# A graph layer's per-step node row, loaded as one row and spread by TensorE

## The reference

```
rel_t_enc = cos((last_update[src] - t)[:, None] * time_w + time_b)
e = concatenate([rel_t_enc, msg]) @ We                   # per edge
q = (x @ Wq + bq)[dst];  k = (x @ Wk + bk)[src] + e
alpha = sum(q * k, per head) / sqrt(64)
a = softmax of alpha over the edges of one dst
out = segment_sum((v[src] + e) * a, dst) + x @ Wskip + bskip
x = layernorm(x + out)
```

## Time and profile before

| | us |
|---|---|
| median of 3 runs | 12,685.32 (12,684.47 to 12,685.91) |
| profiled execution, its own time | 12,758.32 |
| its span, first to last instruction | 12,756.5 |
| busy in the span: POOL / PE / DVE / ACT | 9104.8 / 8280.4 / 7035.3 / 4268.4 |

### The profile page before, as it was taken

The page is one execution under the profiler, slowest core; times in us unless marked ns, Lnnn a source line. Parts: engine busy times, 40 slices in busy tenths (PEclk is TensorE's granted clock), DMA queues, the critical chain, the costliest instruction groups (busy, mean ns, idle before and its releaser), DMA issues.

```text
span 12756.5 us, 215589 instructions
## 1 busy us (share of the span) xinstructions
PE 8280.4 (65%) x44603; PEld 7400.1 (58%) x44604; DVE 7035.3 (55%) x23935; ACT 4268.4 (33%) x14084; POOL 9104.8 (71%) x7644
## 2 busy tenths in 40 slices
PE   5777777777777777777645555555555555555555
PEld 2666666666666666666635555555555555555555
DVE  4776776777777777767763333333333333333334
ACT  1444444444444444444422222222222222222221
POOL 2666666666666666666468888888888888888884
PEclk8777877787777777777766666666666666666667
DMA  6555555555555555555533333333333333333335
GB/s 184 150 149 146 148 149 149 148 152 148 150 148 148 150 152 150 148 149 149 135 37 35 35 35 35 35 35 35 35 35 35 35 35 35 35 35 35 35 35 120
DMA packets 1699357, 1205.64 MB, mean 95 GB/s; under 512 B 749995, under 2 KB 1471983, under 8 KB 1699023
## 3 DMA queue, kind: packets, MB, share of 16 engines
q0 software_dynamic: 634368, 675.42, 32.8%
q1 hardware_dynamic: 1013840, 503.68, 15.2%
q10 hardware_dynamic: 51072, 25.69, 0.7%
HBM read 924.83 MB, written 279.22 MB: 94 GB/s over the span
## 4 chain that ended last, share of the span: by engine, by line
DMA 22%; issue 20%; POOL 19%; DVE 13%; another core or an unknown queue 9%; PE 8%; DVEq 4%; SPq 3%; ACT 2%; POOLq 0%; ACTq 0%
DMA part_scratch<-kve,idx 21%; POOL part_scratch L609 19%; DVE y_all L1142 3%; PE bank L703 2%; DVE acc L1275 2%; PE bank L694 1%; DVEq L375 1%; PE bank L684 1%; DVEq L273 1%; PE bank L676 1%; DVE ohT L1135 1%; ACT wv L859 1%; DVE oh L1188 1%; DVE oh L1181 1%
## 5 line engine op out<-in xcount | busy, mean ns | idle before, releaser
L609 POOL DMA_INDIRECT part_scratch<-kve,idx x3232 | 5134.7, 1589 | 1056.8 <-issue 884.2
L560 POOL DMA_INDIRECT kv<-kv_scratch,took x3520 | 3544.5, 1007 | 2303.4 <-issue 1366.8
L761 PE MATMUL bank<-ident,kv 128*128 128x128 f32 x3232 | 753.4, 377 | 2403.8 <-DVE ohT L1364 2314.6
L1390 DVE TENSOR_TENSOR idx<-kv,twins 128x4 int32<-128x4 f32 x808 | 131.4, 163 | 3627.2 <-DMA part_scratch<-kve,idx 3627.2
L761 PEld LDWEIGHTS bank<-ident,kv 128*128 128x128 f32 x3232 | 489.4, 188 | 2582.1 <-ACT kv L940 2217.7
L859 ACT ACTIVATE wv<-tables,weights 128x65 f32<-128x65 f32 x7040 | 1771.5, 337 | 3.5 <-PE bank L703 2.5
L771 PE MATMUL bank<-ohT,oh 128*128 128x128 f32 x6464 | 1644.2, 435 | 148.6 <-DVE oh L1356 138.8
L771 PEld LDWEIGHTS bank<-ohT,oh 128*128 128x128 f32 x6464 | 1408.1, 321 | 423.7 <-DVE oh L1356 357.0
L947 ACT ACTIVATE oh<-bank 128x512 f32<-128x512 f32 x808 | 482.4, 597 | 3258.4 <-PE bank L771 3258.3
L703 PE MATMUL bank<-wv,oh 128*128 128x130 f32 x7040 | 1302.3, 342 | 363.4 <-issue 239.3
L1123 DVE TENSOR_TENSOR tables<-kv,bank 128x512 f32<-128x512 f32 x880 | 599.7, 681 | 1682.1 <-remote 1610.8
(11 more groups left out here) (166 smaller groups left out, 9952.4 us busy)
## 6 DMA issues: line engine op xcount, KB each, us to landing
kve<-nodes_scratch SPq DMA_DIRECT2D x880, 256.0 KB
feat<-in_edge_attr_dram SPq DMA_DIRECT2D x880, 96.0 KB
kv<-kv_scratch,took POOLq DMA_INDIRECT x3520
qb<-q_scratch SPq DMA_DIRECT2D x880, 64.0 KB
part_scratch<-kve,idx POOLq DMA_INDIRECT x3232
part_scratch<-zrow SPq DMA_DIRECT2D x220, 128.0 KB
feat<-in_edge_attr_dram SPq DMA_DIRECT2D x880, 32.0 KB
kv<-part_scratch ACTq DMA_DIRECT2D x56, 448.0 KB, 6.0
```

The source lines that it names most:

```text
L560: pool.indirect_dma_start(kv[:, k, g, :], None, kv_d, bass.IndirectOffsetOnAxis(ap=took[:, j, g, 0:1].bitcast(I32), axis=0)).then_inc(s_ga ...
L609: pool.indirect_dma_start(part_d[g], bass.IndirectOffsetOnAxis(ap=idx[:, k, g:g + 1], axis=0), sum_ring[:, k, g, :], None, compute_op=ALU. ...
L761: op = pe.transpose(banks[0][:, g * P:(g + 1) * P], taken[:, st.k, 0, g:g + 1].to_broadcast([P, P]), ident[:, :])
```

## The change

SP loads the node row once, as 512 floats on one partition (`row_in`, two slots in `kve`). PE multiplies a row of ones with it (`row_stage`, one matmul of 512 columns, one ahead of what was the most advanced stage), so that all 128 partitions of a PSUM bank hold the row; ACT copies the bank to `node_row_of` (`rowc_stage`), which now has two slots; DVE's `onehotT_stage` waits for ACT's copy where it waited for the DMA. The PSUM bank comes from the node sums, which keep `banks[6]` alone. PE's sum for a step now waits for DVE's sum of the step just before. Two lists are reordered: PE's `sum_stage` comes after `q_stage`, and DVE's `sum_stage` comes right after `ke_stage`, not last.

```
-                wait(sp, s_oht, st.before(QS))
-                sp.dma_start(node_row_of[:, r, :], nodes_d[...].rearrange("(a n) -> a n", a=1).to_broadcast([P, G * P])).then_inc(s_bc[r], 16)
+                wait(sp, s_row, st.before(2))
+                sp.dma_start(row_in[:, st.k % 2, :], nodes_d[...].rearrange("(a n) -> a n", a=1)).then_inc(s_bc[st.k % 2], 16)
...
+            def row_stage(st):
+                pe.wait_ge(s_bc[st.k % 2], 16 * st.use(2))
+                wait(pe, s_rowc, st.s)
+                pe.matmul(row_ps[:, :], ones[0:1, :], row_in[:, st.k % 2, :], start=True, stop=True).then_inc(s_row, 1)
...
-                wait(pe, s_acc, st.before(2))
+                wait(pe, s_acc, st.s)
...
-                    at(i, k, (feat_stage, 15), (sum_stage, 1), (q_stage, 14), (e_stage, 15))
+                    at(i, k, (feat_stage, 15), (q_stage, 14), (sum_stage, 1), (e_stage, 15), (row_stage, 16))
...
+            def rowc_stage(st):
+                act.wait_ge(s_row, st.s + 1)
+                wait(act, s_oht, st.before(2))
+                act.activation(node_row_of[:, st.k % 2, :], row_ps[:, :], ACT.Copy).then_inc(s_rowc, 1)
...
-                    at(i, k, (featc_stage, 15), (weigh_stage, 2), *sines, *gaps, *exps, *smalls)
+                    at(i, k, (featc_stage, 15), (weigh_stage, 2), *sines, *gaps, *exps, *smalls, (rowc_stage, 16))
...
-                dve.wait_ge(s_bc[r], 16 * st.use(QS))
+                dve.wait_ge(s_rowc, st.s + 1)
...
-                    at(i, k, *turn[0], (ve_stage, 14), *turn[1], (ke_stage, 14), *turn[2], (block_stage, 0), *once(5, forward_stage),
+                    at(i, k, *turn[0], (ve_stage, 14), (block_stage, 0), *turn[1], (ke_stage, 14), *turn[2], (sum_stage, 0), *once(5, forward_stage),
```

More of the change, by code:

```diff
@@ L218, in build @@
         e_ps, q_ps = banks[2:4], banks[4:6]
-        agg_ps = [banks[6 + j][:, 0:HEADS * HB] for j in range(2)]
+        agg_ps, row_ps = banks[6][:, 0:HEADS * HB], banks[7]
         mT_ps, small_ps = banks[0][:, 0:G * ROWS], banks[0][:, 128:128 + 4 * ROWS]
```

17 lines of the change are left out of this document (9 added, 8 removed).

## The result

| | before | after |
|---|---|---|
| median | 12,685.61 us (12,684.47 to 12,686.27, 4 runs) | 12,904.44 us (12,900.53 to 12,911.75, 4 runs) |
| ratio | 1 | 1.0173, 95% interval 1.0156 to 1.0191 |
| profiled execution's span | 12,756.5 us | 12,909.9 us |

The change costs 219 us, or 0.25 us on each of the 880 steps. The direction was forecast; the size was not: the forecast of 13,300 us meant 615 us more than before, 2.8 times what was measured. The profiled execution of before lies 73 us above its median and that of after 7 us above, and the two spans are only 153 us apart; I take sizes from the medians and use the traces for the places.

What follows compares the result with a forecast made beforehand. It took the DVE-PE exchange between gather bursts as the bound. Terms 0.4 + 0.7 + 0.3 = 1.4 us per two steps, 616 us over 880 steps, gave 13,300 us; forecast range 12,900 to 13,650, 8-in-10 range 12,600 to 13,900.

Steps and rivals of the forecast that it cites:

- the feat term: On PE, feature transposes queued behind the row may miss the open part: 1.7 to 2.5 us if so, 0.7 taken.
- period of two steps: POOL gathers two steps in a burst, then the next burst starts: 13.94 us; the forecast added 1.4 us to it.
- The e term: On PE, e starts 1.4 to 2.3 us later, behind DVE's and PE's sums; 0.4 us per period taken.
- 0.74 us of room: Slack between ke's end with POOL's wake-up and POOL's fifth gather, said to absorb part of DVE's 0.6 to 1.5 us loss.
- the open part: Time between gather bursts when PE's results reach other engines promptly and SP's loads start 0.54 us apart.
- second reading: Check of the sum: 6.4 us of PE work and 1.2 to 1.3 us of remaining waits, 7.6 to 7.7 a step.
- The ACT term: On ACT, the row's copy queues ahead of the feature copy PE needs: 0 to 0.6 us per period, 0.3 taken.
- release: Moment a gather burst is through and DVE and ACT, held waiting for PE's results, start at once.
- The SP term: SP waits for PE's row matmul two steps back, with other loads queued behind; costed at 0.
- The closed parts: While gathered rows are in flight, PE's results reach others late and queues creep; SP's loads were 2.86 us apart.
- the door: Image for prompt delivery of PE's results: a gather burst closes it until about 2 us after its last gather's start.
- Rival (c): PE's 1.92 us of idle time takes the row in, so nothing changes: 12,685, at worst some 20 us more; chance 0.10.

Runs made afterwards that it cites:

- one_bank: Kernel before with one PSUM bank for the node sums and both changed orders (PE, DVE), row still broadcast: 12,839.66 us, 1.0043.
- order_only: Kernel before with both changed orders, PE's and DVE's, but two banks for the sums: 12,830.22 us, 1.0043.
- bank_matmul: one_bank plus one spare 512-column matmul a step on PE, waiting for nothing and read by nobody: 12,872.03 us, 1.0145 of the kernel before.
- bank_copy: bank_matmul plus ACT's copy of that bank and the two waits between PE and ACT: 12,886.81 us, 1.0155 of the kernel before.
- four_slots: Changed kernel with four places for the loaded row instead of two, so SP waits for the matmul four steps back: 12,860.85 us, 1.0139 of the kernel before.
- row_early: Changed kernel with PE's row matmul moved ahead of the sum, no longer after e: 12,915.61 us, 1.0186 of the kernel before.
- changed_again: Changed kernel without an edit, run where the kernel before takes 11,749 us: 11,902.64 us, 1.0133.
- order_pe: Kernel before with PE's changed order alone, q ahead of the sum, in a set where the kernel before takes 11,749 us: 11,750.86 us, 1.0001.

## Why the prediction was right and wrong

Right, point by point: slower; the broadcast worth nothing (0.9993, and 1.0174 against 1.0173); the queue's 37 MB gone and DMA at 0.43 where 0.45 was forecast; PE above 80% busy (84%); PE's sum waiting for `acc` over 100 us (115.5); e no longer right behind ke (in the timeline after it starts 3067.21 - 3065.25 = 1.96 us after ke's end, where 1.5 to 2.4 was forecast); ve waiting now also for plain PE results (108.9 us against 8 in the earlier trace rows); the second layer unmoved; gathers no closer together. What was wrong is the size, 615 us for 219, and each of the three terms of the sum was too large. That 12,904 us lies inside the forecast's 12,900 to 13,650, by 4 us, is chance. The step that failed most is the feat term: 0.7 us per period, where all of the row's PE work costs 0.29 (0.20 to 0.39 by the ends of the intervals), since most of it went into PE's idle time. By the ladder of kernels, which mixes sets and whose steps under 0.2% the intervals can't tell from nothing, in the sets with the kernel before at 12,685 to 12,782 us, per period of two steps (1% is 127 us, 0.29 us per period):

| term of the sum | forecast, us per period | measured | from |
|---|---|---|---|
| e later, by DVE's and PE's sums | 0.4 | 0.13 (0.43%), bank and orders together | one_bank, order_only |
| feat after the row | 0.7 | 0.29 (1.02%), the row's PE work with all that it delays | bank_matmul over one_bank |
| ACT's copy ahead of the features | 0.3 | 0.03 (0.10%) | bank_copy over bank_matmul |
| SP's wait, and the rest | 0 | 0.05 (0.18%) | changed kernel over bank_copy |
| sum | 1.4, 616 us | 0.50, 219 us | changed kernel |

**The e term.** The wait came as described, and e started later. The step that failed is that DVE's loss, 0.6 to 1.5 us, would reach POOL past 0.74 us of room. In the example after, POOL's two encoding operations stood in the way of the fifth gather, and ke was early enough by 3072.03 - 0.78 - 3070.51 = 0.74 us. I had taken the room from one burst in which these operations stood elsewhere. And the mechanism was not what the 0.43% is: order_only, without the wait for the bank, costs the same. In the fast sets DVE's order alone costs 0.7% and PE's nothing. I had costed that move, in a sentence on DVE, at nothing, because two operations ahead were more than PE needs to begin; I looked only at PE as the neighbour. In the sets of this sum one more cause is possible that I had not named: POOL's gathers last 1031 ns in one_bank and 1016 in order_only, against 1007 before (1000 to 5000 us). That is 0.10 and 0.04 us a step, and the 0.43% is 0.06. No run separates it from the exchange of DVE and PE.

**The feat term** was the largest and was mis-sized most. I took a third of 1.7 to 2.5 us for the feat that misses the open part. The matmul alone, in the same place ahead of feat, costs 0.29 us per period, with all that it delays. Whether feat's place behind the row is any part of that is not shown: row_early moved the row ahead of the sum and gained nothing (1.0186 against 1.0173), but there it delays e. The check by a second reading failed as well: it set PE's work at 6.4 us a step and left 1.2 to 1.3 of waits on top, so 7.6 to 7.7. The waits are 1.13 us, as said. But PE's work is 840.98/141 = 5.96 us: the row takes 1.27 where I said 1.4, and the other work fell from 5.02 to (840.98 - 179.4)/141 = 4.69 us, at a granted clock of 0.81 against 0.79. It is 4.71 in one_bank too, before any row. So PE's busy time for the same matmuls is not fixed from kernel to kernel, and I added to it as if it were; the clock, 0.79 to 0.83 in these stretches, is too close to explain all of it. That is the larger error of the two: 0.33 us of the half microsecond by which 7.6 was above 7.09.

**The ACT term.** The copy was to delay the feature copy by up to 0.6 us at a release. After, the copy waits for the release in the place of the feature copy and costs 0.03 us per period. That is inside the intervals. Why it is so cheap the runs don't say.

**The SP term** had the opposite sign of error: forecast 0, and four_slots gains 43 us, if the touching intervals are taken at their middles. SP waits 241 us in 1000 ahead of the row's load. The row is not late for PE by it (PE's wait for the load is 27 us in the whole run, in a term that I kept in the range at 0 to 160); which other load is late was not found.

**The closed parts.** I wrote that PE's results come late while gathered rows are in flight. In the fast sets gathers are in flight all the time, POOL being full, and no late release appears, with the same program. So gathers alone don't close the door. What does is not settled by these runs, and it stays open.

**Rival (c)**, that PE's idle time takes the row in, was given 0.10 with the argument that PE waited for `acc` only 22.5 us. For the row's own work it is the nearest to what happened, though the total it named (12,685, at worst some 20 us more) is 199 us below the measured 12,904. one_bank opened a wait for `acc` of 190 us that costs nothing by itself (order_only), and bank_matmul filled half of it. Idle time took in 1.0 us of the first matmul and charged 0.15; it charges 0.40 for the second.

## What to carry to other kernels

An engine's wait that appears with a change need not cost, and the idle time of an engine in a ring of engines can be paid out at a rising price, as here: put a spare instruction of the size in question into the kernel before, with no waits, and measure it, once and twice. The cost of a broadcast load is read the same way, by loading a single partition. When an order is changed, look at every engine that works beside it, not only at those that wait for it: here POOL's own instructions became longer beside DVE's scans. And when two kernels cost the same, see that the same parts make up the total.

## What the runs showed of the hardware that was not expected

- The kernel before takes 11,749 us in some sets and 12,685 to 12,782 in others, bank_matmul's chip being the same one on which changed_again ran at the fast level. The difference is in the first layer: a step takes 5.76 us where the mean from 1000 to 5000 us before is 6.91 (2317 gathers), and 880 times that is 1,010 us; the spans of order_pe and of the kernel before are 1,006 us apart. In the fast sets the releases that the profile calls remote are gone (270 and 311 us of 1000 in the earlier trace rows), and SP's load of features (line 483) is issued in 332 to 368 ns each time, where it took 4 to 725 before (3000 to 4000 us), so the slow stretches of the earlier trace rows are absent; where SP waits for nothing its loads start 0.53 us apart. Why one program has two such levels was not found. The second layer is the same to within 0.1% on POOL: 839.13 us busy of 1000 in order_pe, 839.19 before.
- The change costs 1.73% at the one level and 1.33% at the other, by different engines: mostly PE's work for the row at the first, POOL's longer instructions at the second, where a kernel with a spare 512-column matmul takes as long as one with 16 columns (1.0048 and 1.0047), by different parts.
- A POOL operation of 128 x 8 elements took 1.06 us and one of 128 x 256 elements 1.41 us beside DVE's 16 x 512 scans, against means of 0.22 and 0.62 where none overlaps a scan and DVE is as busy. Gathers beside the second scan took 1.84 to 2.08 us, against 0.95.
- A matmul from one partition over 512 f32 columns costs as much PE time as one from 128 partitions: 1.12 and 2.07 us for its two records in two places of the timeline, against 1.10 and 1.92 in the earlier trace rows.
